# Row maxima that run 16 instead of 20 ahead, the shift's piece an iteration later, and stores moved to ScalarE's queue

## The reference

```python
x = x + xattn(layernorm(x), ctx_512)      # xattn, for every batch and head:
    att  = where(causal, q @ k.T * scale, -inf);  y  = softmax(att) @ v
    attc = qc @ kc.T * scale;                     y += softmax(attc) @ vc
    return y @ Wp + bp
x = x + ffn(layernorm(x))                 # ffn:
    scores = (tanh(xf @ gate_w.T) + 1) * 0.5
    vals, idx = top_k(scores.T, k)        # k = 512 tokens for each of 8 experts
    h = gelu(layernorm(xf[idx]) @ fc1 + b1);  o = (h @ fc2 + b2) * vals
    return xf.at[idx].add(o)
```

## Time and profile before

| | |
|---|---|
| three plain runs | 1584.35, 1579.7, 1584.2 us |
| the profiled execution | 1579.36 us, its span 1577.6 us |
| busy TensorE, VectorE, ScalarE, GpSimd | 1498.1, 1123.5, 911.0, 548.3 us |
| prologue up to the first exponential | 68.6 us |
| 32 units | 68.6 to about 1242 us |
| a unit in the middle | 36.4 to 38.6 us |

### The profile page before, as it was taken

How to read it: one execution, slowest core, us unless ns; L and a number is a source line. 1 busy time by engine, 2 the same in 40 slices (tenths; PEclk the granted TensorE clock), 3 DMA queues, 4 the chain that set the end, 5 groups by cost and what they waited for, 6 DMA issues and landing times. The chain is left out here.

```text
span 1577.6 us, 26522 instructions
## 1 busy us (share of the span) xinstructions
PE 1498.1 (95%) x9036; PEld 730.0 (46%) x9036; DVE 1123.5 (71%) x3069; ACT 911.0 (58%) x1754; POOL 548.3 (35%) x1012
## 2 busy tenths in 40 slices
PE   8899999999999999999999999999999967999997
PEld 4443443445344444444454445344443433676674
DVE  6878887877787788778887887787883166455451
ACT  2177777677767777677777777767767401112111
POOL 4122333442444235233433442343213211443442
PEclk9599999999999999999999999999999988999999
DMA  6776661955286547746572856185500120444443
GB/s 135 157 134 106 128 93 69 127 109 107 92 117 117 98 103 122 125 93 105 119 120 88 113 119 110 70 116 114 85 3 3 41 85 14 124 92 120 117 97 51
DMA packets 82490, 155.46 MB, mean 99 GB/s; under 512 B 13012, under 2 KB 46420, under 8 KB 82356
## 3 DMA queue, kind: packets, MB, share of 16 engines
q1 hardware_dynamic: 76212, 145.25, 47.6%
q0 software_dynamic: 6144, 8.52, 3.2%
HBM read 96.52 MB, written 53.08 MB: 95 GB/s over the span
## 5 line engine op out<-in xcount | busy, mean ns | idle before, releaser
L829 ACT ACTIVATE probs<-bank_ps 128x512 f32<-128x512 f32 (+1 forms) x1408 | 730.3, 579 | 243.7 <-PE bank_ps L613 235.0
L920 DVE TENSOR_REDUCE chunk_max<-bank_ps 128x1 f32<-128x512 f32 x1024 | 653.6, 683 | 139.8 <-PE bank_ps L652 135.9
L652 PE MATMUL bank_ps<-k_stack,q_stack 62*128 62x512 f32 (+3 forms) x1536 | 533.5, 430 | 7.4 <-DVE chunk_max L920 4.1
L613 PE MATMUL bank_ps<-q_stack,k_stack 64*128 64x512 f32 (+3 forms) x1536 | 510.7, 421 | 25.5 <-ACT probs L829 22.6
L652 PEld LDWEIGHTS bank_ps<-k_stack,q_stack 62*128 62x128 f32 x1536 | 246.7, 190 | 370.7 <-DVE chunk_max L920 200.6
L923 DVE CUSTOM_DVE_ANT_0 masked<-bank_ps,causal 128x128 bf16<-128x128 f32 (+3 forms) x512 | 232.9, 485 | 62.2 <-PE bank_ps L652 58.7
L631 PE MATMUL out_ps<-probs,v_cross 128*32 128x512 f32 x2048 | 275.1, 609 | 0.0
L613 PEld LDWEIGHTS bank_ps<-q_stack,k_stack 64*128 64x128 f32 x1536 | 233.3, 188 | 82.6 <-ACT probs L829 76.2
L1093 POOL TENSOR_TENSOR pool_idle<-pool_idle 128x1 f32<-128x1 f32 x292 | 56.8, 194 | 579.4 <-ACT probs L829 383.9
L1418 ACT ACTIVATE h<-h_ps,b1T 128x512 f32<-128x512 f32 x64 | 44.0, 687 | 240.4 <-PE h_ps L1354 125.4
L1369 PE MATMUL o_ps<-w2T,h 128*128 128x256 f32 x512 | 114.6, 380 | 3.3 <-DVE o L1520 3.1
(11 more groups left out here) (165 smaller groups left out, 1365.7 us busy)
## 6 DMA issues: line engine op xcount, KB each, us to landing
parts_dram<-parts SPq DMA_DIRECT2D x70, 512.0 KB, 2.7
k_stack<-parts_dram SPq DMA_DIRECT2D x180, 192.0 KB, 11.5
q_stack<-parts_dram SPq DMA_DIRECT2D x180, 128.0 KB, 10.6
w1T<-in_L_ffn_fc1s SPq DMA_DIRECT2D x8, 1024.0 KB, 5.0
w2T<-in_L_ffn_fc2s SPq DMA_DIRECT2D x8, 1024.0 KB, 7.4
z_rows<-z_sb SPq DMA_DIRECT2D x8, 528.0 KB, 3.1
x_sb<-in_x SPq DMA_DIRECT2D x8, 512.0 KB, 3.8
ctxT<-in_ctx SPq DMA_DIRECT2D x8, 512.0 KB, 4.8
```

The source lines that it names most:

```text
L613: mm = pe.matmul(bank_of(turn)[:, of.at:of.end], k_stack[base:base + SIDE, g, pair, of.keys:of.keys + P], q_stack[base:base + SIDE, g, pai ...
L652: return pe.matmul(bank[:, 0:n], q_stack[base:base + MAX_ROWS, g, pair, qc:qc + P], k_stack[base:base + MAX_ROWS, g, pair, k0:k0 + n], sta ...
L829: nc.scalar.activation(probs[:, buffer(u, i, p), side, columns], bank_of(("score", g, i, p, side))[:, columns], ACT.Exp, scale=SCALE)\
L920: nc.vector.tensor_reduce(dst, bank[:, 0:n], AX.X, ALU.max).then_inc(max_done, 1)
```

## The change

Three edits. `LEAD` is 48 + 16, and in `PLAN` the piece `shift` stands in iteration 8 of each unit instead of 7. The last maximum of a unit now falls into iteration 7 instead of 6. In (0, 8) the shift now stands ahead of yT1, in (2, 8) ahead of qc, and in (3, 8) ahead of zT1; in (3, 7) zT0 stands alone. Second, the five stores of the second half are issued by ScalarE, in the prologue behind its last bias activation. Third, the two DMAs of the rows of ones stand ahead of the first `fill_directly` on SyncE.

```diff
-LEAD = N_A + 20
+LEAD = N_A + 16
...
-    (0, 5): (("vc1", 1),), (0, 6): (("yT0", 0),), (0, 7): (("shift", 0),), (0, 8): (("yT1", 0),),
+    (0, 5): (("vc1", 1),), (0, 6): (("yT0", 0),), (0, 8): (("shift", 0), ("yT1", 0)),
...
             sp.wait_ge(k_clear, 2)
+            sp.wait_ge(ones_set, 1)
+            for side in range(SIDES):
+                rows = k_stack[SIDE * side + MAX_ROWS:SIDE * side + SIDE].rearrange("p s h n -> p (s h n)").bitcast(F32)
+                sp.dma_start(rows.rearrange("p (c n) -> p c n", n=T),
+                             ones_row[0:SHIFT_ROWS].unsqueeze(1).broadcast_to(
+                                 [SHIFT_ROWS, UNITS * UH // SIDES * K_COLS // T, T])).then_inc(ones_in, 16)
...
-            for name in HALF_PIECES:
-                store_parts(prologue_piece(PROLOGUE.index((name, 1))))
-            sp.wait_ge(ones_set, 1)
-            for side in range(SIDES):
...
             put_shift(0, 0)
...
+            def store_parts(piece):
+
+                a, e = COL[piece.name]
+                act.wait_ge(*halves_ready(piece))
+                act.dma_start(parts_dram[piece.half, :, :, a:e].rearrange("t c n -> c t n"), parts_of(piece).bitcast(F32))\
+                    .then_inc(parts_out, 16)
...
                 elif n == ALONE:
+                    for name in HALF_PIECES:
+                        store_parts(prologue_piece(PROLOGUE.index((name, 1))))
                     act.wait_ge(v_bias_done, 1)
```

More of the change, by code:

```diff
@@ L71 @@
     (0, 1): (("out_cross", 0),), (0, 2): (("v", 1),), (0, 3): (("out_self", 0),), (0, 4): (("vc0", 1),),
[9 rows of a table removed]
[4 rows of a table added]
+    (2, 4): (("out_cross", 0),), (2, 5): (("out_self", 0),), (2, 6): (("vc0", 0),), (2, 8): (("shift", 0), ("qc", 1)),
+    (2, 10): (("k", 1),), (3, 0): (("kc0", 1),), (3, 1): (("kc1", 1),), (3, 2): (("v", 0),),
+    (3, 4): (("out_cross", 0),), (3, 5): (("out_self", 0),), (3, 6): (("vc1", 0),), (3, 7): (("zT0", 0),),
+    (3, 8): (("shift", 0), ("zT1", 0)), (3, 9): (("gate", 0),),
 }
```

## The result

The changed kernel takes 1600.47 us (median of four runs, 1596.93 to 1602.17) against 1584.28 of before (four runs as well): ratio 1.0107, 95% interval 1.0083 to 1.0132. Its profiled execution took 1596.93 us, span 1595.0, so 17.4 us more span than before.

The account below looks back on a forecast made before the run. TensorE paces the units, VectorE close behind; VectorE's maxima pace the prologue and two DMAs bound its ends. +0.3 + 0.5 - 0.6 + 6.3 - 2.0 + 1.2 = +5.7 on 1579.4, plus 1: 1586 us, range 1576 to 1598.

Parts of the forecast that it names:

- The rows of ones: Prologue's start: early ones occupy two engines, so first fills land at 31.0 us (29.4 to 33.6), 3.7 us later.
- The stores: Prologue, on ScalarE's queue: free 4.6 us of SyncE, run beside the last fills with over 6 us of room; counted nothing.
- The clock: Prologue's first value pieces: TensorE idles longer and its clock may fall earlier; +0.5 us, range 0 to 1.7.
- The end of the prologue: First tile of batch 0 needs only the 61st maximum: at most 3.4 us sooner; with the fills' delay, +0.3 us net.
- Unit 1: Its first scores' wait of 0.61 us for the shift's rows disappears: -0.6 us.
- (0, 8): Group 0, iteration 8: yT1 behind the shift clashes over the low half; 0.9 us, 7 times, +6.3 (2.8 to 7.7).
- (2, 8): Group 2, iteration 8: qc behind the shift covers the low half; 0.3 us less, 7 times, -2.0 (0 to -3).
- (3, 7) and (3, 8): Group 3, batches 1 to 6: the clash moves from zT0 to zT1; 0 to 0.4 us more each, +1.2.
- Rival 3: VectorE becomes the bound in iteration 7, which keeps 3.1 to 3.3 us; 0.4 more in 31 units, +12: 1598; chance 0.17.
- The sum: Whole kernel: +0.3 + 0.5 - 0.6 + 6.3 - 2.0 + 1.2 = +5.7 us.
- Rival 1: Prologue wins (fills landed at 29.4 us) and the clash in (0, 8) stays small: 1576.5 us; chance 0.25.
- rival 2: Prologue: ones first, slower; fills end at 33.6 or later and the clock falls early, +4.5 us: 1589.7; chance 0.13.

Follow-up runs that it names:

- 1: The kernel before with only the two DMAs of ones moved ahead of the first fills on SyncE: 1593.94 us, ratio 1.0056.
- 7: The kernel before with only the ones moved early, but issued from ScalarE's queue while SyncE issues the fills: 1587.11 us, ratio 1.0031.
- 12: The kernel before with only unit 0's rows of ones (2 x 24 KB) ahead of the first fills, the rest in their old place: 1585.48 us, ratio 1.001.
- 2: The kernel before with only the five stores moved from SyncE to ScalarE: 1581.52 us, ratio 0.9992.
- 13: The changed kernel with its stores back on SyncE behind the fills; lead, shift and early ones stay: 1596.12 us, ratio 1.0085.
- 9: The kernel before with lead 16, shift in iteration 8, stores on ScalarE, yT1 in (0, 7), no DMAs of ones (memset to 1.0): 1578.91 us, ratio 0.9962.
- 10: The kernel before without DMAs of ones (memset to 1.0) and with zT0 moved from (3, 7) to (2, 9): 1577.40 us, ratio 0.9950.
- 6: The kernel before without DMAs of ones, k_stack set to 1.0 by its memsets, nothing else changed: 1582.90 us, ratio 1.0003.
- 3: The kernel before with only lead 16 and the shift in iteration 8, ones and stores as before: 1589.86 us, ratio 1.0043.
- 4: The changed kernel with the ones back behind the fills on SyncE; lead, shift and stores stay changed: 1585.32 us, ratio 1.0016.
- 8: As 4, with yT1 in iteration (0, 7) instead of behind the shift in (0, 8): 1583.24 us, ratio 1.0010.
- 11: As 8, with one maximum's tile fewer in iteration 7 and one more in iteration 6 of every unit: 1592.79 us, ratio 1.0048.
- 5: As 4, without DMAs of ones; k_stack is set to 1.0 by the memsets that were there: 1583.18 us, ratio 1.0006.

## Why the prediction was wrong

1586 was forecast, in a range of 1576 to 1598; 1600.5 was measured. The direction "no change" fell with the prologue alone; the units came out near their sum. The first maximum, at 40.39 us, lies past the 34 that I had named as a sign of being wrong.

- **The rows of ones: this step failed.** I let the two engines owe a sixteenth of twelve fills, at bounds of 29.4 and 33.6, and took 31.0. That takes for granted that the fills get issued behind the ones. They do not: SyncE issues a fill only every 1.6 us instead of 0.63, which fits a fill that needs the two busy engines as well as the idle ones (experiments 1, 7, 12). The delay is then nearly the ones' whole time, 5.6 us in the issue beside the 1.5 of their own: first maximum +7.1, beyond my upper bound of 6.3. The row that should have warned me was there: the first shift in the earlier trace rows, read 7.2 us behind its write. I used it for the arrears and not for SyncE. The Trainium skill (DMA: Bandwidth & Descriptors, "Issuing engines are not separate DMA queues") says that all issuers share the same 16 engines and that a second issuer saves only issue time. Experiment 7 agrees on the sharing, with 34.57 us for the first maximum; in 2 not even the issue time was saved.
- **The stores: this step failed too.** I placed them beside the last fills, with 6 us of room, as in the kernel before. With the fills late they ran from 27.2 us beside the six key fills on which the first maximum waits: 9.26 us instead of 3.75, +5.9 on the first maximum (the changed kernel against 13). Alone they are harmless (2). The two edits had to be priced together: the first moved the fills to where the second put its 2.6 MB. Nor did they free SyncE's 4.6 us.
- **The clock: this term was too small.** I gave +0.5, at most 1.7. From the first maximum to the first shift it took 32.2 us instead of 29.9: +2.3. The bound was made from a dip of 3.4 us, while the clock stayed down for the whole first value piece (3.78 instead of 2.05 us). In 12 an idle time of 3.40 us ahead of the first maximum instead of 1.85 went with a fall at 30.7 us instead of 39.6, and with 3.5 us lost; in 13 the clock stayed at half for 58 us and 5 were lost. Between first maximum and first shift TensorE was at half clock for 17.6 us before, 22.0 in the changed kernel and in 1, 31.6 in 12 and 34.9 in 13; the delays are 0, 2.3, 2.3, 3.5 and 5.0. VectorE gets its tiles later from a slower TensorE: it is busy 5.13 of 8.60 us in 12, and 8.18 of 8.50 before (columns as in the earlier trace rows; 12 first):

```profile
31.00:39.60 8.60, 7.89 (x31) 5.66 (x29) 5.13 (x13) 1.17 (x2) 0.00 (x0) 0.50 0.72 121
```
```profile
31.00:39.50 8.50, 7.46 (x33) 4.46 (x33) 8.18 (x23) 1.17 (x2) 0.00 (x0) 1.00 0.73 121
```

- **The end of the prologue.** I forecast up to 3.4 us from the lead and read the 1.33 us of the earlier trace rows as a wait for DMA, since VectorE "had freed its bank". It had not: the first tile of batch 0 takes the bank of the tile two, not four, before it. In the changed kernel its weight load starts, at 80.69, 0.12 us behind the end of the last but one maximum (the third of the four from 78.69: 79.89 + 0.68 = 80.57); so it needs the 63rd of 64, not the 61st. With nothing else in the way the lead is worth 2.3 us (9 against 10). The ones' waiting shift costs 0.2 us with a lead of 20 (6), where VectorE ends later anyway. With a lead of 16 it is what the first scores wait for: the first exponential comes 2.8, 1.5, 2.3 and 1.9 us behind the first tile's weight load in 3, 4, 8 and 11, against 0.9 wherever the ones were early or gone (5, 9, 13 and the changed kernel).
- **Unit 1.** Its wait for the rows is gone as forecast; unit 0 lasts 39.74 us instead of 40.25.
- **(0, 8)** was right: 0.84 more in a unit of group 0 (0.9 forecast), mostly from the clash (8 against 4: 0.61 of it goes with yT1). But 0.29 us in it are yT1's wait for a score bank, which I had not counted, and there were 16 waits for the low half, not 13.
- **(2, 8)** was wrong in sign: 4.73 instead of 4.20, and 0.16 more in the unit where -0.3 was forecast. The four products of qc do cover the low half (no wait for it there), but the shift takes one more of three score banks, and qc waits 0.30 us for the first exponential, as yT1 does above.
- **(3, 7) and (3, 8)**: 7.40 became 7.52, +0.1 (+0.2 forecast).
- **Rival 3** was half right: iteration 7 keeps 3.13 us without a piece, and iteration 8 gets the shift on top. But iteration 9 gives 0.23 back, so a unit pays 0.13 to 0.16, not 0.4. Its reason, VectorE alone, did not stand (11).
- **The sum** of the units without unit 1's wait, +5.5, stands beside 3.6 in the one pair of traces, in which dips of the clock fell differently, and beside 6.8 (4.1 to 9.5) by ratio for lead and shift alone (3), prologue included. Batches without a dip give 0.6 (batch 2) and 1.2 (batch 6), or 4 to 8 in seven.
- **Rival 1** took the lower bound of the early ones and **rival 2** the upper one; the true cost lay beyond both. Rival 2 named the right place, with 4.5 us for what was 13.

## What to carry to other kernels

A DMA whose destination spans few partitions is cheap only where nothing urgent is issued behind it, from any queue: here it occupied two engines for 7.6 us (an estimate from 192 KB at the 26 GB/s of the earlier trace rows), and the fills issued behind it, on SyncE's queue in 1 and beside it in 7, came out at less than half their pace. Ask first whether it is needed: here a memset that ran anyway wrote the same constant. Two edits that each only shift a transfer must be priced in the order that results from both. And pieces that take a bank from a short rotation should stand in iterations of their own: moving one transpose, with the ones' DMAs gone, made the kernel 0.5% faster (10; 0.2 to 0.7), where the whole change made it 1.1% slower. The two faster kernels, 9 and 10, each have a transpose moved and no DMAs of ones; either alone gave nothing that can be told (5, 6 and 8).

## What the runs showed that I had not expected

- **SyncE's issue held up by another queue's DMA**: 8.88 us for six DMAs that otherwise take 3.75, with the ones on ScalarE's queue (7). While the ones move in the changed kernel, the other fourteen engines are mostly idle (DMA share 0.12, 0.25, 0.35 above).
- **Where runs of one kernel differ.** Most dips to half clock fall into (3, 9), behind the gate's 128x8 products, and one lasts 3.4 or 6.8 us. In 3, 4 and 13 one falls at 98 to 109 us instead, in (0, 8) of batch 0, and unit 0 takes 41.9 to 42.1 us there, 39.2 to 40.6 in the others. In experiment 1, batch 3:

```profile
668.30:675.00 6.70, 6.70 (x33) 3.25 (x29) 4.22 (x10) 3.44 (x9) 2.34 (x8) 0.50 0.63 207
```
```profile
667.83 0.87 ACT L829 ACTIVATE probs<-bank_ps 128x384 f32<-128x384 f32 x2 [0.47 <-PE bank_ps L613]
670.23 1.76 ACT L829 ACTIVATE probs<-bank_ps 128x384 f32<-128x384 f32 x4 [0.50 <-PE bank_ps L613]
674.29 2.06 ACT L829 ACTIVATE probs<-bank_ps 128x512 f32<-128x512 f32 x4 [2.30 <-PE bank_ps L613]
```

  (3, 10) takes 4.06 us there (670.23 to 674.29), in experiment 7 without a dip 2.72:

```profile
667.85 1.64 ACT L823 ACTIVATE probs<-bank_ps 128x384 f32<-128x384 f32 x4
670.57 2.06 ACT L823 ACTIVATE probs<-bank_ps 128x512 f32<-128x512 f32 x4 [1.08 <-PE bank_ps L607]
```

  With (3, 9) a dip of 6.8 us costs about 2, one of 3.4 about 1.2. The trace of 1 has three of the long and one of the short in batches 2 to 5, that of 7 two short ones: 5 of the 7.4 us between their spans (1593.56 and 1586.12). What decides which a run gets stays open.
